# A windowed-attention block on one core: the four engines' hand-written order replaced by a new one, and where a bias is added

## The reference, cut to what matters

```python
h = _ln(x, g1, b1)                                   # normalise each token
h = jnp.roll(h, (-3, -3), axis=(1, 2)); xw = _win_part(h)
q, k, v = split(xw @ w_qkv + b_qkv)
attn = softmax(q * HD ** -0.5 @ k.T + bias[rel] + MASK)
out = (attn @ v) @ w_proj + b_proj
x = shortcut + roll(_win_rev(out), (3, 3))
h2 = _ln(x, g2, b2)
h2 = gelu(h2 @ w_fc1 + b_fc1, approximate=False) @ w_fc2 + b_fc2
return x + h2
```

## Time and profile before

| | |
|---|---|
| runs shown | 3275.57, 3276.84, 3277.97 us; median 3276.84 |
| the profiled execution | 3275.45 us, its span 3273.7 us |
| PE busy | 3117.6 us, 95% |
| DVE busy | 2814.3 us, 86% |
| ACT busy | 2283.0 us, 70% |
| POOL busy | 1316.7 us, 40% |
| the granted TensorE clock | 0.999 of full speed |
| DMA | mean 34 GB/s, 12.4% of the 16 engines' time for loads and stores |

### The profile page before, as it was taken

How to read it: one execution, slowest core, us unless ns; L and a number is a source line. 1 busy time by engine, 2 the same in 40 slices (tenths; PEclk the granted TensorE clock), 3 DMA queues, 4 the chain that set the end, 5 groups by cost and what they waited for, 6 DMA issues and landing times.

```text
span 3273.7 us, 121784 instructions
## 1 busy us (share of the span) xinstructions
PE 3117.6 (95%) x51984; PEld 2750.4 (84%) x51984; DVE 2814.3 (86%) x7463; ACT 2283.0 (70%) x4478; POOL 1316.7 (40%) x775
## 2 busy tenths in 40 slices
PE   5999999999999999999999999999999999999998
PEld 4888888888888888888888888888888888888887
DVE  6888888888888888888888888888888888888885
ACT  3667766776777677767776777677767776776675
POOL 2344434443444444344434443444344434443442
PEclk9999999999999999999999999999999999999999
DMA  1111111111111111111111111111111111111110
GB/s 51 34 32 37 36 33 32 37 37 32 32 36 37 32 34 35 37 32 36 33 37 32 36 32 37 32 37 32 37 32 37 34 35 32 37 34 34 32 27 22
DMA packets 217584, 111.95 MB, mean 34 GB/s; under 512 B 15094, under 2 KB 216790, under 8 KB 217046
## 3 DMA queue, kind: packets, MB, share of 16 engines
q1 hardware_dynamic: 216899, 104.14, 12.4%
q10 hardware_dynamic: 147, 0.02, 0.0%
HBM read 52.73 MB, written 51.38 MB: 32 GB/s over the span
## 4 chain that ended last, share of the span: by engine, by line
DVE 43%; ACT 30%; PE 16%; issue 10%; SPq 0%; POOL 0%; DMA 0%; DVEq 0%; POOLq 0%; ACTq 0%
DVE stream L620 9%; DVE scores L600 8%; DVE row_max L603 8%; ACT hT L460 7%; DVE xn L588 6%; DVE raw L566 5%; ACT L482 5%; ACT qd L444 4%; PE psum L771 4%; ACT probsT L406 4%; PE psum L729 4%; DVE row_sum L613 4%; PE psum L773 3%; PE psum L772 3%; ACT xT L425 2%
## 5 line engine op out<-in xcount | busy, mean ns | idle before, releaser
L858 PE MATMUL psum<-wfc,hT 128*112 128x128 f32 x7168 | 835.6, 274 | 1.0 <-ACT hT L460 0.7
L858 PEld LDWEIGHTS psum<-wfc,hT 128*112 128x112 f32 x7168 | 797.8, 177 | 8.3 <-ACT hT L460 1.0
L356 POOL TENSOR_TENSOR probs<-probs,row_inv 128x784 f32<-128x784 f32 x256 | 389.4, 1521 | 987.1 <-DVE row_inv L615 987.1
L460 ACT ACTIVATE hT<-psum,bias_h 128x392 f32<-128x392 f32 x1024 | 598.8, 605 | 71.1 <-PE psum L773 70.7
L406 ACT ACTIVATE probsT<-psum 128x512 f32<-128x512 f32 x512 | 281.5, 613 | 484.7 <-PE psum L745 484.7
L588 DVE TENSOR_SCALAR xn<-x_in,mean,rstd 112x128 f32<-112x128 f32 x896 | 466.0, 587 | 1.8 <-POOL rstd L376 1.7
L368 POOL TENSOR_TENSOR stream<-stream,brow_fc 112x896 f32<-112x896 f32 x128 | 267.3, 2088 | 485.6 <-DVE xn L588 485.6
L771 PE MATMUL psum<-x2T_hi,wfc_hi 128*128 128x392 f32 x1024 | 448.7, 438 | 2.6 <-DVE x2T_lo L638 1.5
L400 ACT ACTIVATE probs<-scores 128x784 f32<-128x784 f32 x256 | 224.0, 875 | 210.0 <-DVE scores L605 210.0
L444 ACT ACTIVATE qd<-psum,bias_q,parity_one 128x392 f32<-128x392 f32 x512 | 318.4, 674 | 59.0 <-PE psum L773 55.8
L773 PE MATMUL psum<-x2T_lo,wfc_hi 128*128 128x392 f32 x1024 | 348.5, 340 | 0.0
(11 more groups left out here) (78 smaller groups left out, 5869.6 us busy)
## 6 DMA issues: line engine op xcount, KB each, us to landing
x_in<-in_x SPq DMA_DIRECT2D x224, 168.0 KB
out<-stream SPq DMA_DIRECT2D x224, 168.0 KB
x_in<-in_x SPq DMA_DIRECT2D x224, 17.5 KB
out<-stream SPq DMA_DIRECT2D x224, 17.5 KB
x_in<-in_x SPq DMA_DIRECT2D x224, 10.5 KB
out<-stream SPq DMA_DIRECT2D x224, 10.5 KB
x_in<-in_x SPq DMA_DIRECT2D x32, 96.0 KB
out<-stream SPq DMA_DIRECT2D x32, 96.0 KB
```

The source lines that it names most:

```text
L356: pool.tensor_tensor(p, p, r.unsqueeze(2).to_broadcast([128, 2 * WINDOWS, N]), ALU.mult).then_inc(probs_normed, 1)
L460: act.activation(hT[:, chunk, band * BAND:(band + 1) * BAND], tok_psum(FC1 + n)[:, 0:BAND], ACT.Gelu, bias=bias_h[:, chunk:chunk + 1]).the ...
L858: last = pe.matmul(tok_psum(FC2 + h)[0:TOK, (t - t0) * C:(t - t0 + 1) * C], hT[:, chunk, t * TOK:(t + 1) * TOK], wfc2[:, chunk, :], start= ...
```

## The change

The round is rewritten for PE, DVE, ACT and POOL at once. Every task gets semaphores of its own, one for each band, half or piece (`q_made[0]`, `fc1_made[3]`), so that pieces can be made out of their numerical order; waits that another wait already implies are left out. The pipeline is one round deeper at either end (`LEAD, LAG = 3, 3`). Besides the order:

- ACT: the one-column `table_probe` is gone. The `Gelu` table is now loaded where its first user stands, behind `copy_o(0)` and ahead of the piece 2 of the hidden layer. The copies of the transposed probabilities leave out unused columns (4 x 113 in place of 512).
- PE: `transpose_probs` works on 113 rows in place of 128. The hidden pieces come in the order 2, 0, 1, 4, 3, 5, 6, 7.
- POOL: the order in a round is power (second), probabilities of band 0, input plus projection bias, power (first), probabilities of band 1, last bias. The input-plus-bias add no longer follows the power that starts `normalise` of the next input; it waits only for its data. The last bias no longer waits for `xn2_ready`; it stands behind the probabilities of band 1, which wait for `inv_ready[1]`.
- DVE: each normalisation is done in two pieces at different places.

The core of the diff, with the new rounds of POOL, ACT and DVE and the part of PE's on which the prediction works:

```diff
-            def step(at):
-                if at.has():
-                    normalise_probs(at, 0)
-                if at.has(-1):
-                    wait(pool, var2_ready, at.count(1, 1, -1))
-                    pool.tensor_tensor(rstd2[:, :], ve2[:, :], minus_half[:, :], ALU.pow).then_inc(rstd2_ready, 1)
-                    wait(pool, xn2_ready, at.count(2, 2, -1))
-                    pool.tensor_tensor(stream[:, at.slot(-1), :, :], stream[:, at.slot(-1), :, :],
...
+            def step(n):
+                if has(n - 1):
+                    wait(pool, var2_ready, upto(n - 1))
+                    power(rstd2, ve2, rstd2_ready)
+                if has(n):
+                    wait(pool, inv_ready[0], upto(n))
+                    normalise_probs(0)
+                    wait(pool, x_loaded[n % STEPS], dma_count(n % STEPS, n // STEPS))
+                    if has(n - 4):
+                        wait(pool, out_stored[n % STEPS], dma_count(n % STEPS, (n - 4) // STEPS))
+                    add_row(n, x_in, brow_proj, x_biased)
+                if has(n + 2):
+                    if n < 0:
+                        wait(pool, var1_ready, upto(n + 2))
+                    power(rstd1, ve1, rstd1_ready)
+                if has(n):
+                    wait(pool, inv_ready[1], upto(n))
+                    normalise_probs(1)
+                if has(n - 1):
...
+                    add_row(n - 1, stream, brow_fc2, x1_biased)
```

```diff
-                    wait(act, gelu_loaded, at.count(1, 0, -1))
-                    act.activation(table_probe[:, :], bias_h[:, 0:1], ACT.Gelu).then_inc(gelu_loaded, 1)
...
+                if has(n + 1):
+                    copy_v()
+                    wait(act, scores_shifted[1], upto(n + 1))
+                    exp(1)
+                    wait(act, o_made[0], upto(n + 1))
+                    copy_o(0)
+                if has(n):
+                    wait(act, fc1_made[2], upto(n))
+                    gelu(2)
+                    wait(act, x2T_made[1], upto(n))
+                    copy_x2(1)
...
```

```diff
+            def step(n):
+                if has(n - 1):
+                    wait(dve, exp_done[0], upto(n - 1))
+                    inverse_sums(n - 1, 0)
+                if has(n - 3):
+                    wait(dve, fc2_made[0], upto(n - 3))
+                    wait(dve, x1_biased, upto(n - 3))
+                    add_to_stream(n - 3, 0, out_added)
+                if has(n - 1):
+                    wait(dve, v_made[1], upto(n - 1))
+                    copy_v()
+                if has(n - 2):
+                    wait(dve, rstd2_ready, upto(n - 2))
+                    normalise(xn2, stream[:, (n - 2) % STEPS, :, :], mean2, rstd2, xn2_ready, 0)
+                if has(n - 1):
+                    wait(dve, scores_made[1], upto(n - 1))
+                    shift_scores(n - 1, 1)
...
```

In the shapes, `transpose_probs` and `copy_probsT`:

```diff
-                        last = pe.transpose(psum[:, S_BANK + 2 * band + f, 128 * pair:128 * (pair + 1)],
-                                            probs[:, band, f, 2 * pair:2 * pair + 2, :].rearrange("p w m -> p (w m)"),
-                                            ident[:, :])
+                        last = pe.transpose(psum[:, S_BANK + 2 * band + f, 128 * pair:128 * pair + rows],
+                                            probs[0:rows, band, f, 2 * pair:2 * pair + 2, :].rearrange("p w m -> p (w m)"),
+                                            ident[0:rows, 0:rows])
```

More of the change, by code:

```diff
@@ L48 @@
 LOADS = [2 * len(ROLLED), 2 * len(ROLLED), 2 * len(ROLLED), 3 * len(ROLLED)]
+LEAD, LAG = 3, 3
 SCALE = float(HD) ** -0.5
 EPS = 1e-5
[L52 to L71, removed]
-def wait(eng, sem, value):
[L76 to L91, removed]
+def wait(eng, sem, value):
+    if value > 0:
+        eng.wait_ge(sem, value)
 def swin_block(nc, x, g1, b1, w_qkv, b_qkv, w_proj, b_proj, rel_slices, g2, b2, w_fc1, b_fc1, w_fc2,
@@ L96, in swin_block, with has, upto, run_steps @@
     images = x.shape[0]
+    steps = images * STEPS
+    def has(k):
+        return 0 <= k < steps
+    def upto(k):
+        return min(k, steps - 1) + 1
+    def run_steps(step):
+        for n in range(-LEAD, steps + LAG):
+            step(n)
     with ExitStack() as ctx:
@@ L323, in _ @@
                 load(0, s)
-            def step(at):
[L326 to L335, removed]
+            def step(n):
+                if has(n) and has(n + STEPS):
+                    wait(sp, x_biased, upto(n))
+                    wait(sp, xn1_ready[0], upto(n))
+                    wait(sp, xn1_ready[1], upto(n))
+                    load((n + STEPS) // STEPS, n % STEPS)
+                if has(n - 2):
+                    wait(sp, out_added[0], upto(n - 2))
+                    wait(sp, out_added[1], upto(n - 2))
+                    store((n - 2) // STEPS, (n - 2) % STEPS)
+            run_steps(step)
             for s in range(STEPS):
@@ L349, in _, with normalise_probs @@
             pool.wait_ge(brow_ready, 1)
[L351 to L353 removed]
+            def normalise_probs(band):
                 p = probs[:, band, :, :, 0:N].rearrange("p f w m -> p (f w) m")
@@ L388, in _, with power, add_row @@
-            run_steps(pool, images, step)
+                                   ALU.mult).then_inc(probs_normed[band], 1)
+            def power(rstd, ve, ready):
+                pool.tensor_tensor(rstd[:, :], ve[:, :], minus_half[:, :], ALU.pow).then_inc(ready, 1)
+            def add_row(k, src, row, ready):
+                pool.tensor_tensor(stream[:, k % STEPS, :, :], src[:, k % STEPS, :, :],
+                                   row[:, :].unsqueeze(1).to_broadcast([TOK, TILES, C]), ALU.add).then_inc(ready, 1)
@@ L773, in product, with qk_product @@
                 return pe.matmul(made, w_hi, x_lo, start=False, stop=True)
-            def qk_product(at, use, part, band):
+            def qk_product(k, bank, part, band):
+                made = qkvo_psum(bank)[:, 0:BAND]
                 if band == 0:
-                    return pe.matmul(qkvo_psum(use)[:, 0:BAND], wqk[:, part, :], xT[:, at.slot(1) % 2, 0, :, 0:N],
-                                     start=True, stop=True)
-                return product(qkvo_psum(use)[:, 0:BAND], wqk_hi[:, part, :], wqk_lo[:, part, :],
-                               xT_hi[:, :], xT_lo[:, :])
@@ L801, in make_values, with make_q @@
-            def make_values(at, band):
-                if band == 0:
-                    wait(pe, qk_copied, at.count(4, 3))
-                else:
-                    wait(pe, o_copied, at.count(2, 1))
+                    return pe.matmul(made, wqk[:, part, :], xT[:, k % 2, 0, :, 0:N], start=True, stop=True)
+                return product(made, wqk_hi[:, part, :], wqk_lo[:, part, :], xT_hi[:, 0, :],
+                               xT_lo[:, 0, :])
+            def make_q(k, band):
+                qk_product(k, Q_BANK[band], 0, band).then_inc(q_made[band], 1)
@@ L851, in make_out, with make_hidden @@
-            def make_out(at, h):
-                if at.has(-1):
-                    wait(pe, residual_added, at.count(2, h + 1, -1))
+                last.then_inc(proj_made[h], 1)
+            def make_hidden(c):
+                band, chunk = divmod(c, CHUNKS)
+                rows, cols = slice(band * BAND, (band + 1) * BAND), slice(chunk * C, (chunk + 1) * C)
+                product(tok_psum(c)[:, 0:BAND], wfc1_hi[:, cols], wfc1_lo[:, cols], x2T_hi[:, rows],
+                        x2T_lo[:, rows]).then_inc(fc1_made[c], 1)
```

682 lines of the change are left out of this document (319 added, 363 removed).

## The result

The changed kernel takes 3550.46 us (3549.99 to 3551.64, 4 runs) against 3277.4 us: a ratio of 1.083, 95% interval 1.081 to 1.085. It is 8.3% slower. Forecast were 3208 us and a range up to 3365.

A forecast was written before the change was run, and what follows sets the result against it. No engine was full, PE nearest at 95% busy, standing 1.6 us a round. PE's 15.66 plus ACT's 8.77 made 24.43 us, 24.6 with +.2 for collisions; 128 x 24.6 + 58.8 = 3208 us, range 3120 to 3365.

The forecast's parts named there:

- the loop of PE and ACT: PE from hidden piece 5 to `attend` of band 0, 15.66 us, then through ACT and back, 8.77: 24.43 us a round.
- T: Start of hidden piece 5 on PE, from which the prediction counts a round to the next such start.
- PE's own sum: PE's work without waits: 23.5 us a round before, 23.4 if it became the bound in the new order, chance .08.
- The stall on DVE: Input's `normalise` beside POOL's add L384: 1.73 us a round goes, DVE's work falls from 22.0 to 20.3 us.
- I take +.2 us a round for this: Remaining DVE and POOL collisions: band 1's probabilities start about .8 us late, .6 of it slack; 24.6 us a round.
- DVE never lets go between them: One `normalise`'s instructions start .27 us apart and last .34, so POOL cannot get in between; argued against the slower case.
- a sign: If the forecast is right, POOL's adds take longer than 2.1 us, as they wait for DVE.
- Rival A: POOL gets in between DVE's instructions, stalls of 2.1, 1.4 and 1.0 us: 25.7 us a round, 3348 us, chance .28.
- The title's own part: POOL's add L384 moved from beside the input's `normalise` on DVE: stall of 1.73 us a round, 221 us over 128 rounds.
- The narrow transposes: Transposed probabilities with 113 of 128 columns: 2 x .10 us on PE and .13 on each pair of copies.
- The 2.66 us for a switch of tables: ACT's `Gelu` load by the skill, 1283 ns plus about 1380 of drain: 25.8 us a round, 3361 us; given no chance.

The follow-up runs named there:

- where no add collides: Changed kernel; POOL's input add waits for the residual's normalise, its last bias for the variance, DVE's subtractions first: 3113.98 us, ratio .950.
- One wait: Changed kernel with POOL's add of the input waiting until DVE has normalised the first four residual tiles: 3246.57 us, ratio .991.
- the kernel with both waits: Changed kernel; POOL's input add waits for the first four normalised residual tiles, its last bias for the normalised next input: 3142.17 us, ratio .959.

## Why the prediction was wrong

- *The sum's main term, the loop of PE and ACT, held.* 24.43 us were worked out, 23.82 measured where no add collides, with the very chain that was named, the table load on it. It was .6 us too long, most of it on PE: from T (1602.02 in that kernel's chain) to `attend` of band 0 (1617.21) it took 15.2 us and not 15.66, since several distances that I had read across a change from one task to the next are .05 to .12 us shorter in this chain (values .87 and not .96, four tiles .39 and not .50, the second output half 2.62 and not 2.74). That the 1.28 us were on the path was shown by moving them off: .58 us a round came off until PE's own sum stopped it.
- *The step that failed is "The stall on DVE", "I take +.2 us a round for this".* It rested on "DVE never lets go between them". The trace shows the opposite: between two `normalise` instructions, .27 us apart, POOL gets the port whenever it waits. The add did not wait for DVE either: POOL's adds took 2.09 us in the mean, not more as I had named for a sign. The term was not .2 but a change of the bound: DVE stands still 4.9 us a round and sets it at 26.35 us. Rival A described this (chance .28): it had the place, three late tiles of the residual, the .9 us of PE ahead of the second input's transposes (.60 in the trace, PE L687 <- DVE xn L544), and 25.7 us a round.
- *Rival A was .65 us a round too low.* It had the last bias meet the subtraction of the input's rest at 1.0 us, and it met the third input tile, whole, at 1.79 (2.12 less .33); its two other stalls were put a little too high, so that the three made 4.5 us where 4.9 were measured. The rest, .25 us, is idle time of DVE (26.35 less 25.2 busy, where A had .9). That the same piece of `normalise` can be held up by two POOL operations in a row was in no case of mine.
- *No case had the clock.* Behind a wait of 1.54 us in one piece at hidden piece 1, the half clock cost another 1.47 us in two rounds of three. Without it the changed kernel is at 3441 us, still outside the range.
- *The title's own part was read rightly in one half.* Taking the add away from the input's normalise removes 1.73 us of DVE's time, but I never asked whether this time was covered in the old order. It was: behind it in the timeline DVE waits .71 us for the scores, and a DVE that comes earlier only waits longer there.
- *The narrow transposes* were booked at .2 us and gave .1. The 2.66 us for a switch of tables that the Trainium skill gives (ScalarE: Activation LUTs, What ACT_TABLE_LOAD costs) are not seen in any run: in the loop the load is 1.28 us and what follows starts .01 later.

The rule of the Trainium skill that was cited (SBUF — State Buffer, Who interferes with whom) says that the lock is held "for the whole instruction". For POOL's probabilities and adds the trace agrees, and the word that decides is instruction: 1.59 us for the tile behind the probabilities and 2.12 for the tile behind an add. For POOL's power it does not: three `normalise` that ran inside one took .85 us together, as where POOL is idle, so there the measurement decides. Read with care the rule spoke for rival A, since it knows no lock over a run of instructions.

## What to carry to other kernels

Where DVE runs `tensor_scalar` from SBUF to SBUF beside POOL work, count each POOL add or product over a large tensor that can start before the run is over as a stall of its full length (the power was none), and keep them apart by a wait on POOL. Do so for DVE's small `tensor_scalar` too. One wait was worth 304 us here, some 190 of them from the stall and the rest from the half clock that went with it. A stall that shows as a long mean duration is worth only what the engine would not spend waiting right behind it: in the old order 225 us on DVE and nothing of the time. And look at PE's longest standstill in one piece beside the sum of them all: here the half clock came with 1.54 us in one piece and was gone at 1.30, though the sum had grown.

## What the runs showed of the hardware

- POOL gets the port between two DVE instructions that start .27 us apart when nothing is in the way: of a run of three, they took .26, 1.59 and 2.12 us.
- It works the other way as well. In the kernel with both waits POOL's power takes 1.85 us in the mean of both and 2.23 in the one that starts while DVE subtracts the maximum from the scores (two SBUF inputs), against 1.49. The subtraction itself takes 1.18 us, as it starts beside the end of POOL's add (until 1608.64), and .97 where POOL is idle. The three `normalise` inside the power are not held up:

```profile
1608.29 1.18 DVE L566 TENSOR_TENSOR scores<-scores,row_max 128x784 f32<-128x784 f32 x1
...
1608.59 2.23 POOL L316 TENSOR_TENSOR rstd<-ve,minus_half 112x7 f32<-112x7 f32 x1
...
1609.39 0.85 DVE L546 TENSOR_SCALAR xn<-stream,mean,rstd 112x128 f32<-112x128 f32 x3
```

- A `tensor_scalar` of seven elements waits nearly as long as one of 128: 1.97 us for .17.
- Standstills of PE of 1.54 us in one piece were followed by the 1.2 GHz level in 81 of 125 rounds. With the table load moved on the same kernel, the longest was 1.30 us and the sum larger (1.30 + .60 + .49 + .17 = 2.6 us a round, against 1.54 + .60 + .17 = 2.3), and it stayed at 2.4 GHz in nearly every round.
